# Sums of a first expert pass moved from the attention stage into the pass, for 12 of 16 chunks, with the attention stage's first work in the pass's last blocks

## The chip, the cores and the metric

One NeuronCore of one Trainium2 chip. The time is device microseconds of one execution of the whole program. The kernel before has a median of 1704.45 us over three runs (1703.83 to 1704.88).

## What is computed

8192 tokens of 256 features go through a layer norm and a mixture-of-experts block, a layer norm and a spectral attention, and the same expert block again:

```python
def ffn(x):                       # 8 experts, top 2 of a sigmoid router
    shared = silu(xf @ sw1) * (xf @ sw3) @ sw2
    h = gelu(einsum('nd,edh->neh', xf, ew1))
    y = einsum('neh,ehd->ned', h, ew2)
    return shared + einsum('ned,ne->nd', y, comb)
def attn(x):
    q, k, v = x @ Wq.T, x @ Wk.T, x @ Wv.T
    fk, fq = unit(rfft(k)), unit(rfft(q))
    fkv = cumsum(fk * rfft(v), axis=tokens)
    return x + irfft(fkv * conj(fq))
x = x + 0.5 * ffn(layernorm(x))
x = x + attn(layernorm(x))
x = x + 0.5 * ffn(layernorm(x))
```

## The kernel before, in words

The tokens stay in SBUF as `X`, 64 tiles of 128 rows; four tiles are a chunk, so there are 16 chunks (`CH`). The program is written as one instruction stream for each engine, with semaphores between them, and with loops by `run_steps` that peel the first and last steps. Each stream runs the same stages: stage A, stage B, attention, stage A, stage B.

Stage A (`steps_a`) does the shared expert and the router chunk by chunk and scatters each normalised row, with its number, into the list of its expert in DRAM (`lists`).

Stage B (`phase_b`) is the routed experts, the "pass" of this text: 71 pairs of 128-row blocks (`PAIRS`), in an order that follows the tokens, so that the results of early chunks are complete early. For each pair SyncE loads 256 list rows into one of four buffers `XB` (line 345), TensorE transposes them (846), ScalarE and VectorE split them and the expert's weights into a high and a low part, TensorE multiplies in three products (710 to 712), ScalarE applies gelu (616), TensorE multiplies again two steps later, VectorE copies the result out of its bank (1238, `YB`), and GpSimd scatters the rows to `results` in DRAM with two indirect DMAs (453). The instructions of step s on one engine belong to pairs s + 2 (rows and weights), s (first product and gelu) and s − 2 (second product and copy out).

The second pass also adds the results to the tokens. In its step n SyncE waits for the scatter of pair n − 10 and for the sum of tile n − 23, and loads the two results of each token of tile n − 20 into one of four buffers `YT` (`last_part`, line 363). In step n VectorE adds tile n − 19: two multiply-adds of 128x256 (`last_tile`, 1249). ScalarE adds a shift to each tile there, and SyncE stores finished chunks.

The first pass does none of this. Its results are added in the attention stage. There SyncE waits for all scatters (`results_in`), then loads a chunk's results, 1 MB, into the one buffer `YG` (`load_results`, 383). VectorE's attention step s adds chunk s + 2 with eight multiply-adds (1294) and takes its statistics (981, 985). GpSimd makes mean and inverse deviation of them (`rstd_of`, 404 to 418), ScalarE normalises the chunk (676), TensorE transposes it (924), ScalarE and VectorE split it (`XA`), and TensorE makes the spectra of k, v and q of chunk s (710 to 712 on `t_xah`, `t_wfh`). VectorE multiplies k and v spectra, TensorE takes prefix sums over the tokens (934, 936), VectorE multiplies them with the spectrum of q (1326, 1327, 1329), GpSimd finishes the complex product and scales it (499 to 505), TensorE transposes (911) and transforms back (946), and VectorE adds it to `X` (1277).

The order on an engine is as written; nothing is rearranged. Steps −2 and −1 of attention are the start: sums, statistics, normalisation and transposes of chunks 0 and 1. The products of the weights with the Fourier matrix (`attention_weights`, 884) stand on TensorE between the pass and step −1, all twelve in a row:

```python
for i in range(3):
    for m in range(KD):
        for k in range(KD):
            ins = pe.matmul(bank[:, 2 * i + m, 0:D], raw_w[i][:, k, m * P:(m + 1) * P],
                            raw_fwd[:, k, :], start=(k == 0), stop=(k == KD - 1))
```

The raw weights `raw_w` lie where the second pass keeps `YT`; `XN`, `YG` and the other attention buffers lie over stage B's.

## Time and profile before

| what | value |
|---|---|
| median of the runs | 1704.45 us |
| profiled execution, its own time | 1685.51 us |
| its span, first to last instruction | 1683.7 us |
| mean granted TensorE clock | 0.959 |
| PE busy | 1447.3 us (86%) |
| DVE busy | 1289.2 us (77%) |
| ACT busy | 925.0 us (55%) |
| POOL busy | 858.8 us (51%) |
| DMA read and written | 108 GB/s over the span |

Busy times are sums over stages with different limits, so they don't say what a stage waits for. For that the trace is read stage by stage: as windows, which give each engine's busy time in a stretch, and as a timeline, where a row is start, duration, engine, line, operation and operands, and in brackets the idle time before it with what ended it. PE is TensorE, DVE VectorE, ACT ScalarE, POOL GpSimd, SPq the DMA queue of SyncE. A clock of 1.00 is TensorE's full speed.

### The profile page before, as it was taken

How to read it: one execution, taken by the hardware profiler on the slowest of the kernel's cores; microseconds unless marked ns; L12 is line 12 of the kernel's file. 1: busy time of each engine (PE TensorE's matmuls, PEld its weight loads, DVE VectorE, ACT ScalarE, POOL GpSimd, SP SyncE). 2: the span in 40 equal slices, each digit the busy share in tenths (PEclk: the TensorE clock that was granted, in tenths of full speed). 3: DMA queues.
4: the chain of work that ended last, by engine and by line, in shares of the span. 5: the costliest groups of instructions: out<-in, count | busy, mean ns of one | idle time of the engine just before them, and what ended most of it. 6: DMA issues, size and time to landing. Idle time of an engine off the chain costs nothing.

```text
span 1683.7 us, 34493 instructions
## 1 busy us (share of the span) xinstructions
PE 1447.3 (86%) x9656; PEld 1294.3 (77%) x9657; DVE 1289.2 (77%) x3361; ACT 925.0 (55%) x1435; POOL 858.8 (51%) x1056
## 2 busy tenths in 40 slices
PE   1899999998999987688888886999999998999994
PEld 0677777777999887678777775777777788989994
DVE  4788888876666665789999867788888776689887
ACT  3333333335666554688888886333333325677772
POOL 0444444442555554356666655554444432566664
PEclk9999999999999998789999997999999998999997
DMA  8411111124554444311111110111111124578887
GB/s 286 154 50 50 50 51 48 52 69 142 150 152 143 151 140 132 99 29 53 49 51 51 43 38 0 52 53 51 49 48 51 49 77 139 157 235 263 257 255 232
DMA packets 107704, 176.98 MB, mean 105 GB/s; under 512 B 13360, under 2 KB 72632, under 8 KB 107320
## 3 DMA queue, kind: packets, MB, share of 16 engines
q1 hardware_dynamic: 81704, 104.16, 21.7%
q0 software_dynamic: 25920, 71.86, 11.5%
q8 instruction: 37, 0.61, 0.2%
q14 instruction: 43, 0.35, 0.1%
HBM read 95.75 MB, written 86.70 MB: 108 GB/s over the span
## 4 chain that ended last, share of the span: by engine, by line
PE 37%; issue 20%; DVE 16%; POOL 11%; DMA 6%; ACT 5%; SPq 3%; DVEq 1%; another core or an unknown queue 1%; POOLq 0%; ACTq 0%
PE bank L710 10%; PE bank L712 10%; PE bank L711 10%; POOL lists L441 5%; DMA lists<-a_rows,a_slots 3%; PE bank L846 3%; DVE X L1294 2%; ACT a_rows L566 2%; PE bank L946 2%; DVE a_gate_u L1101 2%; ACT a_uh L517 1%; PE bank L934 1%; DVE a_gate_u L1103 1%; DVE a_xtl L974 1%
## 5 line engine op out<-in xcount | busy, mean ns | idle before, releaser
L453 POOL DMA_INDIRECT results<-b_yb,b_goal x284 | 306.9, 1081 | 247.1 <-DVE b_yb L1238 158.1
L441 POOL DMA_INDIRECT lists<-a_rows,a_slots x256 | 256.7, 1003 | 148.5 <-issue 107.5
L517 ACT ACTIVATE a_uh<-a_gate_u 128x512 fp32r<-128x512 f32 x128 | 77.0, 625 | 228.5 <-PE bank L712 196.1
L710 PE MATMUL bank<-a_sw2h,a_uh 128*128 128x256 f32 x512 | 154.5, 302 | 54.0 <-DVE a_xtl L974 41.3
L710 PE MATMUL bank<-b_xbth,b_w1h 128*128 128x256 f32 x568 | 172.8, 304 | 3.6 <-issue 3.3
L710 PE MATMUL bank<-ew_h,b_hth 128*128 x568 | 162.3, 286 | 2.7 <-issue 2.4
L711 PE MATMUL bank<-b_xbtl,b_w1h 128*128 128x256 f32 x568 | 161.5, 284 | 2.9 <-issue 2.7
L712 PE MATMUL bank<-b_xbth,b_w1l 128*128 128x256 f32 x568 | 161.3, 284 | 2.8 <-issue 2.6
L712 PE MATMUL bank<-ew_h,b_htl 128*128 x568 | 160.8, 283 | 2.3 <-issue 2.3
L711 PE MATMUL bank<-ew_l,b_hth 128*128 x568 | 160.8, 283 | 1.8 <-issue 1.8
L974 DVE TENSOR_TENSOR b_htl<-b_hb,b_hth 128x512 fp32r<-128x512 f32 x142 | 97.8, 689 | 80.8 <-ACT b_hth L517 67.5
L711 PE MATMUL bank<-a_sw2l,a_uh 128*128 128x256 f32 x512 | 148.5, 290 | 0.0
L712 PE MATMUL bank<-a_sw2h,a_ul 128*128 128x256 f32 x512 | 148.4, 290 | 0.0
L710 PEld LDWEIGHTS bank<-a_sw2h,a_uh 128*128 128x128 f32 x512 | 101.8, 199 | 60.3 <-DVE a_xtl L974 47.0
L535 ACT ACTIVATE a_gate_u<-bank 128x512 f32<-128x512 f32 x128 | 75.9, 593 | 126.3 <-DVE a_ul L974 74.7
L517 ACT ACTIVATE b_xbth<-bank 128x512 fp32r<-128x512 f32 x142 | 83.7, 589 | 96.4 <-remote 50.0
L710 PE MATMUL bank<-t_wfh,t_xah 128*128 128x256 f32 x384 | 116.1, 302 | 7.6 <-DVE t_xal L974 7.6
L1238 DVE COPY b_yb<-bank 128x512 f32<-128x512 f32 x142 | 97.1, 684 | 32.7 <-remote 29.3
L974 DVE TENSOR_TENSOR a_ul<-a_gate_u,a_uh 128x512 fp32r<-128x512 f32 x128 | 85.0, 685 | 45.6 <-ACT a_uh L517 44.8
L434 POOL COPY a_rows<-tok 128x2 f32 (+1 forms) x64 | 12.3, 193 | 205.3 <-DVE a_slots L1094 205.2
L616 ACT ACTIVATE b_hb<-bank 128x512 f32<-128x512 f32 x142 | 83.9, 591 | 57.9 <-PE bank L712 35.7
L1101 DVE TENSOR_TENSOR a_gate_u<-a_gate_u,bank 128x512 f32<-128x512 f32 x128 | 87.7, 685 | 35.2 <-ACT a_gate_u L535 31.8
(211 smaller groups left out, 4858.3 us busy)
## 6 DMA issues: line engine op xcount, KB each, us to landing
b_xb<-lists SPq DMA_DIRECT2D x142, 264.0 KB
t_yg<-results SPq DMA_DIRECT2D x16, 1024.0 KB, 5.4
b_yt<-results SPq DMA_DIRECT2D x64, 256.0 KB
X<-in_L_attn_x SPq DMA_DIRECT2D x16, 512.0 KB
out<-X SPq DMA_DIRECT2D x16, 512.0 KB
results<-b_yb,b_goal POOLq DMA_INDIRECT x284
lists<-in_c_fill SPq DMA_DIRECT2D x16, 264.0 KB
w_raw_ew<-in_L_ffn_ew SPq DMA_DIRECT2D x2, 2048.0 KB, 13.8
```

The source lines that it names most:

```text
L441: pool.indirect_dma_start(out=lists, out_offset=bass.IndirectOffsetOnAxis(ap=slots[:, q, k, j:j + 1], axis=0), in_=rows[:, q, j, :], in_of ...
L453: pool.indirect_dma_start(out=results, out_offset=bass.IndirectOffsetOnAxis(ap=goal[:, u, blk:blk + 1], axis=0), in_=YB[:, u % 4, blk, :], ...
L517: return act.activation(o, i, ACT.Copy)
L535: act.activation(gate_u[:, m % 2, :], bank[:, 2 + 2 * (m % 2), :], ACT.Sigmoid).then_inc(s_sig, 1)
L616: act.activation(HB[:, par], bank[:, 2 + par, :], ACT.Gelu).then_inc(s_gelu, 1)
L710: pe.matmul(o, a("h"), b("h"), start=first, stop=False)
L711: pe.matmul(o, a("h"), b("l"), start=False, stop=False)
L712: return pe.matmul(o, a("l"), b("h"), start=False, stop=last)
L846: ins = pe.transpose(bank[:, 1 - par, (2 * k + blk) * P:(2 * k + blk + 1) * P], XB[:, slot, blk, k * P:(k + 1) * P], ident)
L974: return dve.tensor_tensor(o, v, h.bitcast(F32), ALU.subtract)
L1101: ch.link(dve.tensor_tensor(gu, gu, bank[:, 2 + 2 * (m % 2), :], ALU.mult))
L1238: dve.tensor_copy(YB[:, slot].rearrange("p b d -> p (b d)"), bank[:, 6 + par, :]).then_inc(s_yok, 1)
```

## The change

`EARLY = 12`. The first pass now loads and adds the results of the first 12 chunks (48 tiles) as the second pass does, without ScalarE's shift and without stores. The attention stage loads and adds chunks 12 to 15 alone; VectorE still takes the statistics of every chunk there, but for chunks 0 and 1. Those have their statistics in steps 67 and 68 of the pass, GpSimd's `rstd_of` after the scatters of pairs 66 and 68, and ScalarE's normalisation into buffers of their own: chunk 0 in ScalarE's step 69, ahead of the last pair's gelu, chunk 1 behind the pass. TensorE's weight products stand in its steps 70 (v, and k once the last gelu has read its bank), 72 (q, once the last result is copied out), the transposes of chunk 0 in step 71. The raw weights are loaded after the last of the 48 tiles is added, since they use its buffers. ScalarE waits for all scatters before its first attention step.

```diff
+EARLY = 12
+WEIGHT_BANK = [2, 4, 6]
-DVE_A, DVE_T, POOL_T, ACT_T = 86, 36, 20, 8
+DVE_A, DVE_T, POOL_T, ACT_T = 86, 22, 20, 8
...
+        XN_FIRST = [place("t", f"xn{i}", [P, J, D], F32, where["yg"] + 4 * i * J * D) for i in range(2)]
+        XAL_FIRST = place("t", "xal_first", [P, KD, N], F32R, where["fq"] + 4 * J * D)
...
-                    if layer:
-                        last_part(n, slot, q)
+                    last_part(n, slot, q)
                 def last_part(n, slot, q):
+                    tiles = TILES if layer else EARLY * J
...
-                        sp.wait_ge(s_ysc[done], (q + (slot + 2) // 4) * 32 + (YW[done] - 32 * (WAY // 4 + 1) + 32))
+                        sp.wait_ge(s_ysc[done], (q + (slot + 2) // 4) * 32 + (YW[done] * layer - 32 * (WAY // 4 + 1) + 32))
-                    if inside(n - LOAD - 4, TILES):
-                        sp.wait_ge(s_fc, n - (LOAD + 3))
+                    if inside(n - LOAD - 4, tiles):
+                        sp.wait_ge(s_fc, n - (LOAD + 3) + EARLY * J * layer)
-                        if slot == 3:
+                        if layer and slot == 3:
...
-                if layer == 0:
-                    run_steps(sp, step, 0, 4, PAIRS - 3, PAIRS, 4)
-                else:
-                    run_steps(sp, step, 0, LOAD + 4, PAIRS - 3, TILES + LOAD + 4, 4)
+                run_steps(sp, step, 0, LOAD + 4, PAIRS - 3, (TILES if layer else EARLY * J) + LOAD + 4, 4)
...
-            run_steps(sp, load_results, 0, 2, CH, CH, 2)
+            sp.dma_start(WI[:], c_inv.rearrange("(k p) n -> p k n", p=P)).then_inc(s_inv, 16)
+            sp.wait_ge(s_atp, 2)
+            for c in range(EARLY, CH):
+                atleast(sp, s_comb, c - EARLY)
+                sp.dma_start(YG[:].rearrange("p j k d -> p j (k d)"), res_d[:, c * J:(c + 1) * J, :]).then_inc(s_yg, 16)
...
+                    if layer == 0 and isinstance(n, int) and n in (PAIRS - 5, PAIRS - 3):
+                        c = (n - (PAIRS - 5)) // 2
+                        rstd_of(c, CH + c + 1, c)
...
+                    if layer == 0 and isinstance(s, int) and s == PAIRS - 2:
+                        act.wait_ge(s_rstd, CH + 1)
+                        act.wait_ge(s_bps, PAIRS - 1)
+                        act.wait_ge(s_goal, PAIRS - 1)
+                        normalised(0, 0, XN_FIRST[0])
...
+            act.wait_ge(s_mm1, PAIRS)
+            attention_weights(0, 1)
+            attention_weights(1, 0)
+            act.wait_ge(s_atp, 1)
+            copy(XA["h"][:], bank[:, 0:2, :]).then_inc(s_ah, 1)
+            act.wait_ge(s_rstd, CH + 2)
...
+            normalised(1, 1, XN_FIRST[1])
+            attention_weights(2, 2)
+            for i in range(4):
+                act.wait_ge(s_ysc[i], YW[i])
-            run_steps(act, attention, -2, 4, CH - 2, CH, 2, ca, ACT_T)
+            run_steps(act, attention, 0, 4, CH - 2, CH, 2, ca, ACT_T)
...
+                    if layer == 0 and isinstance(s, int) and s == PAIRS - 1:
+                        pe.wait_ge(s_mat, 64)
+                        attention_weights(1)
+                        pe.wait_ge(s_gelu, PAIRS)
+                        attention_weights(0)
+                    if layer == 0 and isinstance(s, int) and s == PAIRS:
+                        pe.wait_ge(s_txn, 1)
+                        transposed(XN_FIRST[0])
+                    if layer == 0 and isinstance(s, int) and s == PAIRS + 1:
+                        pe.wait_ge(s_yok, PAIRS)
+                        attention_weights(2)
...
-                    if inside(s - ADD, TILES):
+                    if inside(s - ADD, TILES if layer else EARLY * J):
                         last_tile(s, u, q)
+                    if layer == 0 and isinstance(s, int) and s in (PAIRS - 4, PAIRS - 3):
+                        stats(s - (PAIRS - 4), s - (PAIRS - 4))
+                    if layer == 0 and isinstance(s, int) and s == PAIRS:
+                        weights_low(0, 1)
+                        weights_low(1, 0)
+                    if layer == 0 and isinstance(s, int) and s == PAIRS + 1:
+                        dve.wait_ge(s_ah, 1)
+                        dve.wait_ge(s_yps, PAIRS - 1)
+                        low(XAL_FIRST[:], bank[:, 0:2, :], XA["h"][:]).then_inc(s_al, 1)
...
-                if far:
+                if far and isinstance(s, int) and s + 2 >= EARLY:
                     c = s + 2
-                    dve.wait_ge(s_yg, c * 16 + 16)
+                    dve.wait_ge(s_yg, (c - EARLY) * 16 + 16)
...
-                    stats(c, par)
+                if far:
+                    stats(s + 2, par)
...
-            run_steps(dve, attention, -2, 4, CH - 2, CH, 2, ch, DVE_T)
+            run_steps(dve, attention, 0, 4, EARLY - 2, CH, 2, ch, DVE_T)
```

VectorE, the end of a step in the loop of the first pass: `b_htl` is the low part of the gelu's output, `b_yb` the result copied out, `b_goal` the row numbers, `b_yt` a tile's loaded results. Before:

```order
L1218 ISA x2
L1220 ISA [waits h1_ps]
L1220 COPY b_w1l<-ew_l 128x512
L974 TENSOR_TENSOR b_htl<-b_hb,b_hth 128x512 [waits ht_h]
L1238 COPY b_yb<-bank 128x512 [waits y_out1,y_ps]
L1240 CAST b_goal<-b_xb 128x2
L1213 REGISTER_ALU
```

Now:

```order
L1012 TENSOR_TENSOR b_htl<-b_hb,b_hth 128x512 [waits ht_h]
L1276 COPY b_yb<-bank 128x512 [waits y_out1,y_ps]
L1278 CAST b_goal<-b_xb 128x2
L1285 REGISTER_ALU
L1288 ISA [waits f_in0]
L1288 SCALAR_TENSOR_TENSOR X<-b_yt_108,gates,X 128x256
L107 REGISTER_ALU
L1288 ISA [waits dve_chain]
L1288 SCALAR_TENSOR_TENSOR X<-b_yt_108,gates,X 128x256
```

Two multiply-adds stand behind the result's copy, the first behind a wait for the tile's load, the second behind a wait for the first.

ScalarE, from the last but one pair of the first pass on: `b_hb` is the gelu, `b_hth` its high part, `t_wfh` the high part of a weight product, `t_xn` a normalised chunk, `t_xah` its transposed high part. Before:

```order
L616 ACTIVATE b_hb<-bank 128x512 [waits ht_l,h1_ps]
L517 ACTIVATE b_hth<-b_hb 128x512 [waits y_ps,gelu_ok]
L616 ACTIVATE b_hb<-bank 128x512 [waits ht_l,h1_ps]
L517 ACTIVATE b_hth<-b_hb 128x512 [waits y_ps,gelu_ok]
L517 ACTIVATE t_wfh<-bank 128x256 [waits mat_ps] x6
L676 ACTIVATE t_xn<-X,shift,rstd 128x256 [waits rstd_ok]
L676 ACTIVATE t_xn<-X,shift,rstd 128x256 x3
L517 ACTIVATE t_xah<-bank 128x1024 [waits a_xt_ps]
```

Now:

```order
L638 ACTIVATE t_xn_102<-X,shift,rstd 128x256 [waits goal_ok,xb_ps,rstd_ok]
L638 ACTIVATE t_xn_102<-X,shift,rstd 128x256 x3
L616 ACTIVATE b_hb<-bank 128x512 [waits ht_l,h1_ps]
L517 ACTIVATE b_hth<-b_hb 128x512 [waits y_ps,gelu_ok]
L517 ACTIVATE t_wfh<-bank 128x256 [waits mat_ps,h1_ps]
L517 ACTIVATE t_wfh<-bank 128x256 [waits mat_ps] x3
L517 ACTIVATE t_xah<-bank 128x1024 [waits a_xt_ps]
L638 ACTIVATE t_xn_103<-X,shift,rstd 128x256 [waits goal_ok,xb_ps,rstd_ok]
L638 ACTIVATE t_xn_103<-X,shift,rstd 128x256 x3
L517 ACTIVATE t_wfh<-bank 128x256 [waits mat_ps] x2
L651 ACTIVATE t_sq<-bank 128x1024 [waits y_out3,y_out2,k_ps,y_out1,y_out0]
```

Chunk 0 is normalised ahead of the last pair's gelu, and the first square of the attention stage waits for the four scatter semaphores besides its spectrum.

VectorE, from the copy of pair 68 on: `t_wfl` and `t_xal` are low parts, `t_yg` is a chunk's loaded results. Before:

```order
L1238 COPY b_yb<-bank 128x512 [waits y_out0,y_ps]
L1238 COPY b_yb<-bank 128x512 [waits y_out1,y_ps]
L1238 COPY b_yb<-bank 128x512 [waits y_out2,y_ps]
L974 TENSOR_TENSOR t_wfl<-bank,t_wfh 128x256 [waits mat_hi] x6
L1294 SCALAR_TENSOR_TENSOR X<-t_yg,gates,X 128x256 [waits dve_chain,yg_in]
L1294 SCALAR_TENSOR_TENSOR X<-t_yg,gates,X 128x256 x3
```

Now:

```order
L1276 COPY b_yb<-bank 128x512 [waits y_out0,y_ps]
L1276 COPY b_yb<-bank 128x512 [waits y_out1,y_ps]
L1012 TENSOR_TENSOR t_wfl<-bank,t_wfh 128x256 [waits mat_hi] x4
L1276 COPY b_yb<-bank 128x512 [waits y_out2,y_ps]
L1012 TENSOR_TENSOR t_xal_first<-bank,t_xah 128x1024 [waits y_ps,a_xt_h]
L1012 TENSOR_TENSOR t_wfl<-bank,t_wfh 128x256 [waits mat_hi] x2
```

The low parts of the weights stand between and behind the last copies, chunk 0's low part is there before the attention steps, and no sum stands behind them.

## Rows read from the trace of the kernel before

**Rows 1.** Timeline, DVE: copies of pairs 0, 19, 57, 70, both passes
```profile
407.53 0.68 DVE L1238 COPY b_yb<-bank 128x512 f32<-128x512 f32 x1
...
474.24 0.68 DVE L1238 COPY b_yb<-bank 128x512 f32<-128x512 f32 x1
...
615.93 0.69 DVE L1238 COPY b_yb<-bank 128x512 f32<-128x512 f32 x1
...
657.33 0.69 DVE L1238 COPY b_yb<-bank 128x512 f32<-128x512 f32 x1 [1.03 <-issue]
...
1415.87 0.68 DVE L1238 COPY b_yb<-bank 128x512 f32<-128x512 f32 x1
...
1485.46 0.68 DVE L1238 COPY b_yb<-bank 128x512 f32<-128x512 f32 x1
...
1619.70 0.68 DVE L1238 COPY b_yb<-bank 128x512 f32<-128x512 f32 x1
...
1663.49 0.69 DVE L1238 COPY b_yb<-bank 128x512 f32<-128x512 f32 x1 [0.61 <-remote]
```

**Rows 2.** Windows, pairs 19 to 57, both passes: busy us (instructions), PEclk, DMA share
```profile
474.00:616.00 142.00, 134.07 (x1082) 129.87 (x1081) 90.72 (x192) 86.24 (x154) 79.16 (x77) 0.99 0.48 143
1485.00:1620.00 135.00, 126.96 (x1054) 123.56 (x1053) 122.91 (x268) 104.06 (x190) 89.38 (x76) 1.00 0.86 259
```

**Rows 3.** Source view, line 1249, second pass: ns min/median/max
```profile
L1249 DVE SCALAR_TENSOR_TENSOR X<-b_yt,gates,X x128: 471/484/487, 1479.6 to 1679.7; 128x256 f32 x72, 128x256 f32<-128x256 f32 x56
```

**Rows 4.** Timeline, all engines, 651 to 688 us: the pass to the spectrum
```profile
651.86 1.44 POOL L453 DMA_INDIRECT results<-b_yb,b_goal  x1 [2.31 <-DVE b_yb L1238]
...
652.78 0.60 ACT L616 ACTIVATE b_hb<-bank 128x512 f32<-128x512 f32 x1 [1.04 <-PE bank L712]
...
657.13 3.19 PE L884 MATMUL bank<-b_raw_fwd,b_raw_w 128*128 128x256 f32 x14
...
663.76 0.96 POOL L453 DMA_INDIRECT results<-b_yb,b_goal  x1 [0.31 <-issue]
...
665.64 0.39 ACT L517 ACTIVATE t_wfh<-bank 128x256 fp32r<-128x256 f32 x1 [1.75 <-remote]
...
672.01 3.38 DVE L1294 SCALAR_TENSOR_TENSOR X<-t_yg,gates,X 128x256 f32<-128x256 f32 x8 [5.53 <-DMA t_yg<-results]
...
677.09 0.38 DVE L985 BATCH_NORM_AGGREGATE mv<-st 128x2 f32<-128x6 f32 x4 [0.15 <-DVE st L981]
...
680.35 2.07 ACT L676 ACTIVATE t_xn<-X,shift,rstd 128x256 f32<-128x256 f32 x4 [14.32 <-POOL shift_a L418]
...
682.48 1.97 PE L924 MATMUL bank<-cst,t_xn 128*128 128x128 f32 x8 [20.00 <-ACT t_xn L676]
...
686.17 1.19 DVE L974 TENSOR_TENSOR t_xal<-bank,t_xah 128x1024 fp32r<-128x1024 f32 x1
...
687.51 0.55 PE L710 MATMUL bank<-t_wfh,t_xah 128*128 128x256 f32 x1 [3.07 <-DVE t_xal L974]
```

**Rows 5.** Timeline, DVE, line 1329, one product each attention step
```profile
742.52 1.23 DVE L1329 TENSOR_TENSOR t_fq<-bank,t_fq 128x1024 f32<-128x1024 f32 x1
...
763.64 1.22 DVE L1329 TENSOR_TENSOR t_fq<-bank,t_fq 128x1024 f32<-128x1024 f32 x1
...
784.63 1.23 DVE L1329 TENSOR_TENSOR t_fq<-bank,t_fq 128x1024 f32<-128x1024 f32 x1
...
805.59 1.22 DVE L1329 TENSOR_TENSOR t_fq<-bank,t_fq 128x1024 f32<-128x1024 f32 x1
...
973.88 1.23 DVE L1329 TENSOR_TENSOR t_fq<-bank,t_fq 128x1024 f32<-128x1024 f32 x1
...
993.65 1.23 DVE L1329 TENSOR_TENSOR t_fq<-bank,t_fq 128x1024 f32<-128x1024 f32 x1
```

**Rows 6.** Timeline, DVE, line 1294, eight sums within one step
```profile
790.64 4.57 DVE L1294 SCALAR_TENSOR_TENSOR X<-t_yg,gates,X 128x256 f32 x4
795.37 1.92 DVE L1294 SCALAR_TENSOR_TENSOR X<-t_yg,gates,X 128x256 f32 x4 [0.15 <-DVE X L1294]
```

More of the change, by code:

```diff
@@ L490, in attention @@
                     meanwhile()
-                if far:
+                if far and not (isinstance(s, int) and s < 0):
                     rstd_of(par, s + (CH + 3), s + 2)
@@ L821, in steps_a, with attention_weights, transposed @@
                 return step
+            def attention_weights(i):
+                for m in range(KD):
+                    for k in range(KD):
+                        ins = pe.matmul(bank[:, WEIGHT_BANK[i] + m, 0:D], raw_w[i][:, k, m * P:(m + 1) * P],
+                                        raw_fwd[:, k, :], start=(k == 0), stop=(k == KD - 1))
+                    ins.then_inc(s_mps, 1)
+            def transposed(xn):
+                for k in range(KD):
+                    for j in range(J):
+                        ins = pe.transpose(bank[:, k, j * P:(j + 1) * P], xn[:, j, k * P:(k + 1) * P], ident)
+                ins.then_inc(s_atp, 1)
             def phase_b(layer):
@@ L921, in attention @@
                     atleast(pe, s_ph, s - 1)
[L922 to L925 removed]
+                    transposed(XN_FIRST[1] if isinstance(s, int) and s == 0 else XN)
                 if prev:
@@ L938, in attention @@
                 if old:
+                    if isinstance(s, int) and s == 2:
+                        pe.wait_ge(s_inv, 16)
                     pe.wait_ge(s_ph, s - 1)
```

80 lines of the change are left out of this document (33 added, 47 removed).

## The prediction

> **What bounds the kernel now.** I began with the page: TensorE is busy for most of the span, so a change matters only where TensorE waits or where another engine sets the pace. Then I read the two expert passes and the attention stage between them apart, since their limits differ.
>
> In the expert passes TensorE sets the pace. The source view of the copy that ends a pair gives the clock of a pass: the first pass takes 657.33 − 407.53 = 249.8 us for 71 pairs, the second 1663.49 − 1415.87 = 247.6 us [rows 1]. The windows over pairs 19 to 57 say why this is a good comparison [rows 2]. In the first pass VectorE is busy 90.7 of 142 us. In the second, which already adds one tile of results per step, it is busy 122.9 of 135 us, and TensorE 127.0 of 135. So the second pass is a full trial of what the change does to the first.
>
> Between the pass and the first spectrum the bound is a chain in which TensorE has nothing to do [rows 4]. The weight products begin at 657.13, the last is copied at 665.64. The loaded results hold VectorE back for 5.53 us, the sums take 3.38, statistics end near 677.5, ScalarE normalises from 680.35 (it had waited 14.32 us), TensorE stands 20.00 us before the transposes at 682.48, and the first spectrum starts at 687.51. That is 687.51 − 657.13 = 30.4 us, of which some 10 are TensorE work.
>
> In the attention stage one product per step marks the cadence [rows 5]: 21.12, 20.99 and (784.63 to 805.59) 20.96 us. In the steady steps that is VectorE in order: the eight sums take 795.37 + 1.92 − 790.64 = 6.65 us of each [rows 6]. At 973.88 a step starts that has no sums, because no chunk is left; it takes 993.65 − 973.88 = 19.77 us. So taking 6.65 us from VectorE saves little over 1 us of time: the next limit is a ring of the product, GpSimd's four multiplications, TensorE's transposes, two spectra and prefix sums, and back to the product.
>
> **The change part by part.**
>
> *Start of attention.* Two chunks' loads, sums, statistics and normalisation leave the chain; the weight products stay on TensorE but stand between the last pairs. Count forward from the first pass's end. GpSimd scatters pair 66 from 651.86, and the last ten scatters fill 651.86 to 664.72, 1.29 us each [rows 4]; so pair 66 is out near 654.5. Then its new work for chunk 0 follows; before, ScalarE started 680.35 − 677.09 − 0.30 ≈ 2.9 us after the statistics' last part, so 657.4. ScalarE's normalisation takes 2.07, to 659.5. The last pair's gelu, before at 652.78, is queued behind it on ScalarE: it is 6.7 us late, and its high and low parts (0.6 us for the gelu, a like time for each part) end near 661.3. TensorE has meanwhile done the first four weight products (a third of 657.13 to 665.6, so 2.8 us) and idles some 3 us for that gelu; then 2.8 for the second third, 1.5 for pair 69, 1.5 for the transposes (1.97 in the row), 1.5 for pair 70, 0.7 for the copy, 2.8 for the last third: 660.2 + 2.8 + 1.5 + 1.5 + 1.5 + 0.7 + 2.8 = 671.0. The 1.5 for a pair's second product is an estimate: a pair of 3.5 us is two such products and a few transposes. ScalarE's and VectorE's parts of chunk 0 (VectorE's is 1.19) are done beside this. The first spectrum starts at 671 to 674 instead of 687.51: 13.5 to 16.5 us less; I take **15**. The ends: if GpSimd and ScalarE were never late, TensorE work alone would end at 657.1 + 8.5 + 1.5 = 667 (20 us less); if the weights' load, which now waits for the last tile's sum because it shares its buffers, or the statistics in steps 67 and 68 (1.8 us each on VectorE) push TensorE back by 3 us, and GpSimd is 3 us later, 677 (10 less).
>
> *Scatters.* GpSimd's two new pieces delay the last four pairs' scatters by up to 5.8 us, to about 670.5. ScalarE's first square now waits for them all, but needs the first spectrum anyway: 24 products, as many as a pair has, so 3.5 us at least, to 675. It costs nothing, with some 3 us of cover for the landing of the last scatter; what goes beyond counts one for one.
>
> *Attention steps.* The sums leave the steps for chunks 2 to 11, ten steps. The first two start-up steps are led by ScalarE and gain nothing. In the next two, the one of 21.12 among them, VectorE waited for TensorE before the product, so they were on the ring already: nothing. The six after that go from 20.97 to the ring's length, 1.2 us less by the bare step of 19.77, and a little more in every second one, which has one prefix product fewer: **8 us**. At the least 4, if the statistics and GpSimd's piece for the chunk to come, which the bare step lacks, lie in the ring; at the most ten steps of 1.4, 14. Chunks 12 to 15 keep their sums and their 20.96, and their loads now start long before they are wanted: zero.
>
> *Sums in the pass.* 48 tiles of two sums: 96 × 0.484 = 46.5 us of VectorE [rows 3] in a pass where it has 142 − 90.7 = 51 idle over pairs 19 to 57 alone. The same 38 pairs take 1619.70 − 1485.46 = 134.2 us in the second pass against 615.93 − 474.24 = 141.7 in the first [rows 1]: with sums they are 7.5 us faster, not slower. I don't know why the first pass has a slower last part, so I do not count on losing it. The second pass's first 19 pairs are 2.9 us slower (69.6 against 66.7), which may be its longer code or its own extra work. I take **3 us less**, with the ends 10 less and 8 more.
>
> The trace holds a warning about one cost that would count against this placing. The first four sums in a step take 4.57 us, the next four 1.92, so 1.14 against 0.48 us for the same instruction; the slow ones stand beside GpSimd's two-input operations. In the second pass, beside GpSimd's scatters, the sum is 0.484 at the median and 0.487 at most [rows 3], while a scatter grows from 79.16/77 = 1.03 to 89.38/76 = 1.18 us [rows 2]. The Trainium skill (SBUF — State Buffer, Who Contends for the ports) has VectorE instructions with two SBUF inputs contend with a GpSimd instruction that reads SBUF, the second to issue blocking until the first ends. By it, with each scatter held for a whole sum, a pair would need 2 × (1.29 + 0.484) = 3.55 us of GpSimd, as long as a pair lasts, and the 3 us of the pass would go from the sum. The trace shows a hold of 0.15 us per scatter, a third of a sum: two scatters at 1.29 + 0.15 make 2.9 us per pair, under 3.5, so it stays hidden.
>
> *Sum.* 15 + 8 + 3 = 26 us. The profiled execution has a span of 1683.7 and its own time of 1685.5; the median of the runs is 1704.45, 19 us above it, and I take the difference off the median: **1678 us**.
>
> **The rivals.**
>
> *A, 54%:* as above, 1678.
>
> *B, the steps don't get shorter, 15%:* the statistics, which stay, and what they start on GpSimd keep the ring at 21. For: two of the steps with sums were already on the ring. Against: the bare step of 19.77. 1704.45 − 15 − 3 = 1686.
>
> *C, the pass takes on the second pass's rhythm, 14%:* 7 to 8 us instead of 3 there, and the start at its better end: 1704.45 − 8 − 8 − 18 = 1670.
>
> *D, the start gains half, 8%:* the late gelu, the weights' load and the scatters add up, 7 us instead of 15: 1686. It would show as TensorE idle over 8 us near the weight products.
>
> *E, slower, 5%:* the queue of list loads. SyncE now waits in each step, ahead of the next pair's load, for the scatter of ten pairs before and for the sum of the tile 23 steps before. If VectorE, over 90% busy, falls behind, loads start late, TensorE waits, and VectorE waits for TensorE in turn. It ends slower when it eats the other parts' 23 us and 3.4 more, 0.55 us on each of 48 pairs: 3.73 (141.7/38) becoming 4.28. Against: the second pass has the same queue with output stores on top, DMA share 0.86, and 3.53 per pair. At 4.4 it would give 1704.45 + 32 − 23 = 1713.
>
> *F, no effect beyond the noise, 4%:* the same, stopping at about 4.2 per pair: 1704. A measurement of this kernel tells some 0.2%, 3.4 us, from no change.
>
> The Trainium skill (DMA: Bandwidth & Descriptors, Bandwidth) asks for transfers of 1 MiB or more, against the 256 KiB loads that take the place of twelve of 1 MiB. By its fit of 2.0 us plus size, four small ones cost 10.4 us where one large costs 4.4, an estimate from that page; the sum would change only if they were waited for, and the fit has no wait in it. That mechanism is rival E.
>
> **How the numbers follow.** Forecast 1678. A's own range is 1668 to 1688 by the ends above, not all met at once. B, C and D lie inside 1664 to 1691; leaving out E, F and the tails of A and B is under 2 in 10. Faster 0.91 (A to D), same 0.04 (F), slower 0.05 (E).
>
> **What would show it.** Right: from pair 57's copy to the first spectrum 55 to 58 us where it was 687.51 − 615.93 = 71.6; TensorE's longest idle moment there 3 to 4 us, before the products that need the last gelu, not 20; six steps at 19.3 to 19.8 us and four at 21; the 71 pairs in 240 to 252 us; scatter rows near 1.15 us. Wrong: pairs above 4 us, list loads that TensorE waits for in the first pass, steps still at 21 without sums, or a square that waits for scatters.

## The result, and the profile after

| | before | after |
|---|---|---|
| median of four runs each | 1704.14 us (1703.08 to 1704.88) | 1655.93 us (1649.84 to 1668.29) |
| ratio, 95% interval | | 0.9748 [0.9709, 0.9788] |
| span of the profiled execution | 1683.7 us | 1666.5 us |
| PE, DVE busy | 1447.3, 1289.2 us | 1446.4, 1263.3 us |

The change gains 48 us, 22 more than forecast, and the time lies outside the range of 1664 to 1691. The profiled execution of the changed kernel is its slowest, and that of the kernel before lies 18 us under its timed runs, so their spans differ by 17 us only. Places are therefore read here, not totals, and both kernels were taken again (below).

Timeline, DVE: the copies of pairs 0, 19, 57 and 70 in both passes, as [rows 1].

```profile
410.07 0.68 DVE L1276 COPY b_yb<-bank 128x512 f32<-128x512 f32 x1
...
478.70 0.68 DVE L1276 COPY b_yb<-bank 128x512 f32<-128x512 f32 x1
...
609.67 0.69 DVE L1276 COPY b_yb<-bank 128x512 f32<-128x512 f32 x1
...
660.13 0.69 DVE L1276 COPY b_yb<-bank 128x512 f32<-128x512 f32 x1 [0.27 <-PE bank L733]
...
1382.76 0.68 DVE L1276 COPY b_yb<-bank 128x512 f32<-128x512 f32 x1
...
1460.78 0.68 DVE L1276 COPY b_yb<-bank 128x512 f32<-128x512 f32 x1
```

Pairs 19 to 57, which carry the sums, take 131.0 us instead of 141.7. Pairs 0 to 19 of the second pass, which the change doesn't touch, take 78.0 us instead of 69.6: something varies by 8 us on its own.

Windows over those pairs, as [rows 2], and the source view of the sums, as [rows 3]:

```profile
479.00:609.00 130.00, 125.76 (x1049) 123.22 (x1050) 120.86 (x265) 88.92 (x151) 88.60 (x76) 1.00 0.79 231
```

```profile
L1288 DVE SCALAR_TENSOR_TENSOR X<-b_yt,gates,X x224: 470/483/490, 472.9 to 1662.5; 128x256 f32 x72, 128x256 f32<-128x256 f32 x40
```

VectorE is busy 120.9 of 130 us, the sums cost 0.483 us as forecast, and a scatter 88.60/76 = 1.17 us on average.

Timeline, all engines, from the pass to the attention stage, as [rows 4]:

```profile
646.68 1.89 PE L847 MATMUL bank<-b_raw_fwd,b_raw_w 128*128 128x256 f32 x8
...
650.15 2.07 ACT L638 ACTIVATE t_xn<-X,shift,rstd 128x256 f32<-128x256 f32 x4 [5.88 <-POOL shift_a L415]
...
652.13 0.57 ACT L616 ACTIVATE b_hb<-bank 128x512 f32<-128x512 f32 x1
...
652.75 3.12 PE L847 MATMUL bank<-b_raw_fwd,b_raw_w 128*128 128x256 f32 x8 [4.18 <-ACT b_hb L616]
...
657.65 1.03 PE L854 MATMUL bank<-cst,t_xn 128*128 128x128 f32 x8
...
660.88 1.99 PE L847 MATMUL bank<-b_raw_fwd,b_raw_w 128*128 128x256 f32 x8 [0.78 <-DVE b_yb L1276]
...
662.52 0.47 PE L731 MATMUL bank<-t_wfh,t_xah 128*128 128x256 f32 x1
...
664.87 0.96 POOL L450 DMA_INDIRECT results<-b_yb,b_goal  x1 [0.30 <-issue]
...
667.42 1.02 ACT L651 ACTIVATE t_sq<-bank 128x1024 f32<-128x1024 f32 x1 [4.12 <-DMA results<-b_yb,b_goal]
```

The forecast's picture is there: the normalisation waits for GpSimd, the last gelu stands behind it, TensorE waits 4.18 us for that gelu. From pair 57's copy to the first spectrum it is 662.52 − 609.67 = 52.9 us, against 71.6 before. The first square waits for the scatters, which the forecast had called covered. It comes 4.8 us after the first spectrum, against 5.0 us before, so this wait adds nothing here.

Timeline, DVE, the product of each attention step, as [rows 5]: three in a row.

```profile
754.80 1.22 DVE L1383 TENSOR_TENSOR t_fq<-bank,t_fq 128x1024 f32<-128x1024 f32 x1
...
775.94 1.23 DVE L1383 TENSOR_TENSOR t_fq<-bank,t_fq 128x1024 f32<-128x1024 f32 x1
...
795.78 1.23 DVE L1383 TENSOR_TENSOR t_fq<-bank,t_fq 128x1024 f32<-128x1024 f32 x1
```

Steps without sums alternate: 21.14 and 19.84 us. Windows over the same place in two neighbouring steps show why. Columns: busy PE, PEld, DVE, ACT, POOL, then PEclk.

```profile
760.00:762.00 2.00, 0.06 (x1) 0.00 (x0) 2.00 (x5) 1.90 (x2) 2.00 (x3) 1.00 0.00 0
...
763.00:764.00 1.00, 1.00 (x7) 1.00 (x6) 0.00 (x0) 0.99 (x2) 0.92 (x3) 0.50 0.00 0
...
781.00:783.00 2.00, 0.43 (x4) 0.23 (x2) 2.00 (x5) 1.53 (x2) 2.00 (x2) 1.00 0.00 0
...
784.00:785.00 1.00, 1.00 (x11) 1.00 (x10) 0.00 (x0) 0.60 (x1) 0.99 (x2) 1.00 0.00 0
```

In both steps TensorE stands for some 2 us (2.01 and 1.77) until GpSimd has finished the product. In the first, the granted clock is 0.50 (1.2 GHz) right behind that, and one us holds 7 matmuls instead of 11; in the second it stays at 1.00 (2.4 GHz).

### The profile page after: what moved, and what is told of

The parts are those of the page before. It is cut to its first block, busy times and chain, and to the rows that moved or that the text cites. A ratio compares the mean times of both kernels' runs of the same rounds, so it can differ in the third digit from the quotient of the medians.

```text
span 1666.5 us, 34750 instructions
## 1 busy us (share of the span) xinstructions
PE 1446.4 (87%) x9656; PEld 1293.6 (78%) x9657; DVE 1263.3 (76%) x3361; ACT 927.6 (56%) x1435; POOL 854.6 (51%) x1056
## 4 chain that ended last, share of the span: by engine, by line
issue 25%; PE 25%; DVE 14%; POOL 12%; SPq 9%; ACT 7%; DMA 6%; another core or an unknown queue 1%; ACTq 0%; POOLq 0%; DVEq 0%
PE bank L731 7%; PE bank L733 6%; PE bank L732 6%; POOL lists L438 6%; DMA lists<-a_rows,a_slots 3%; ACT a_rows L566 2%; SPq L348 2%; SPq L367 2%; SPq L349 2%; DVE a_gate_u L1139 2%; PE bank L985 2%; DVE X L1347 2%; PE bank L880 1%; DMA b_xb<-lists 1%; ACT a_uh L517 1%
## 5 line engine op out<-in xcount | busy, mean ns | idle before, releaser
L450 POOL DMA_INDIRECT results<-b_yb,b_goal x284 | 314.4, 1107 | 247.2 <-DVE b_yb L1276 147.2
L616 ACT ACTIVATE b_hb<-bank 128x512 f32<-128x512 f32 x142 | 84.0, 592 | 73.1 <-PE bank L733 51.8
L1288 DVE SCALAR_TENSOR_TENSOR X<-b_yt,gates,X 128x256 f32 (+1 forms) x224 | 107.1, 480 | 18.0 <-DMA b_yt<-results 6.1
L431 POOL COPY a_rows<-tok 128x2 f32 (+1 forms) x64 | 12.2, 190 | 208.3 <-DVE a_slots L1132 208.2
```

The source lines that it names most:

```text
L450: pool.indirect_dma_start(out=results, out_offset=bass.IndirectOffsetOnAxis(ap=goal[:, u, blk:blk + 1], axis=0), in_=YB[:, u % 4, blk, :], ...
L616: act.activation(HB[:, par], bank[:, 2 + par, :], ACT.Gelu).then_inc(s_gelu, 1)
L1288: ins = dve.scalar_tensor_tensor(xt, YT[slot][:, k * D:(k + 1) * D], gates[:, k, bass.ds(t, 1)], xt, ALU.mult, ALU.add)
```

## The experiments

**Both kernels again, one part alone, and a quarter of the sums.** Four kernels side by side; the kernel before took 1703.61 us beside them, and the ratios are to that.

> The kernel before, unchanged, to see where an ordinary execution of it spends the 19 us by which the median lay above the profiled one. Theory R (rhythm): they lie in the expert passes, so this profile, if its time is near 1704, has 71 pairs of the first or the second pass in 258 us or more, with pairs of about 4.0 us, and the attention stage as before (first product at line 1329 to the last 312 us). Theory S (start and steps alone explain the gain): passes of 247 to 251 us, and the 19 us elsewhere. Ratio 1.00.

> The changed kernel, unchanged. Theory R: the first pass is again 248 to 252 us in every profile, with pairs of 3.35 us where tiles are summed, and what differs between executions is the second pass (248 to 265). Theory S: the first pass varies as much as the second. Ratio 0.965 to 0.978.

`sums_only` moves the sums and leaves statistics, normalisation, transposes and weight products of the start behind the pass:

```diff
-                    if layer == 0 and isinstance(s, int) and s in (PAIRS - 4, PAIRS - 3):
-                        stats(s - (PAIRS - 4), s - (PAIRS - 4))
...
-            run_steps(dve, attention, 0, 4, EARLY - 2, CH, 2, ch, DVE_T)
+            run_steps(dve, attention, -2, 4, EARLY - 2, CH, 2, ch, DVE_T)
```

> Only the sums of 12 chunks moved; statistics, normalisation, transposes and weight products of chunks 0 and 1 stand behind the pass as before. Lost against the changed kernel: the interleaved start, of which the wait for loaded results is still gone (13 us of the 25 kept). Theory R: 1704 less 13 (no load and sum at the start), 6 (steps) and about 18 (a regular first pass), 1667. Theory S: 1704 - 13 - 6 = 1685.

`three_chunks` keeps the new start and moves three chunks (the loops that this touches are adapted, which is left out here):

```diff
-EARLY = 12
+EARLY = 3
```

> The start as changed, but sums of only 3 chunks in the pass (tiles in steps 19 to 30); the other 13 chunks are summed in attention steps. Theory R: the pass keeps its irregular rhythm from step 31 on, so 1704 less 25 (start) is 1679, with a first pass as in the kernel before. Theory S: the first pass does not matter, the start gives 25 and the steps nothing: 1679 too, but then sums_only is 1685. The attention steps are back at 20.96 us.

| | median us | ratio to before |
|---|---|---|
| b_again | 1700.25 | 0.9985 [0.9956, 1.0014] |
| a_again | 1660.15 | 0.9755 [0.9722, 0.9788] |
| sums_only | 1668.37 | 0.9802 [0.9769, 0.9836] |
| three_chunks | 1674.29 | 0.9835 [0.9801, 0.9868] |

sums_only takes 1668 us, where theory R said 1667 and theory S 1685; three_chunks, for which both said 1679, takes 1674. The profiles of b_again and a_again (spans 1699.6 and 1659.3 us) are a fair pair. Between the copies of pairs (p) and the products of the attention steps:

| stretch, us | b_again | a_again | difference |
|---|---|---|---|
| p0 to p19 | 68.0 | 71.7 | +3.7 |
| p19 to p57 | 148.7 | 131.3 | −17.4 |
| p57 to first product | 103.1 | 83.9 | −19.2 |
| first to last product | 312.5 | 308.0 | −4.5 |
| last product to second pass | 382.7 | 382.2 | −0.5 |
| second pass, p0 to p70 | 253.5 | 251.9 | −1.6 |

So 17 us come out of the pass itself, where the change only adds work. Moving the sums alone brings it (sums_only has 130.5 us for p19 to p57); with three chunks the pairs come evenly in steps 19 to 30 alone (134.9 us for all 38). Here is what stands in these pairs. View of waits, TensorE, 480 to 600 us, of b_again; then of the changed kernel:

```profile
PE bank L710 <- issue: 4.1, 5, 1.1
PE bank L712 <- issue: 3.5, 5, 1.1
PE bank L711 <- issue: 2.8, 6, 1.0
```

```profile
PE bank L880 <- DMA b_xb<-lists: 2.7, 4, 0.9
PE bank L880 <- issue: 0.8, 3, 0.4
```

In the kernel before TensorE stands 10.4 us between matmuls of one and the same product, with nothing that the profile shows to wait for. Timeline of b_again, one such place, four matmuls that follow one another:

```profile
491.75 0.37 PE L712 MATMUL bank<-b_xbth,b_w1l 128*128 128x256 f32 x1 [0.43 <-issue]
493.18 0.36 PE L710 MATMUL bank<-b_xbth,b_w1h 128*128 128x256 f32 x1 [1.06 <-issue]
493.88 0.28 PE L711 MATMUL bank<-b_xbtl,b_w1h 128*128 128x256 f32 x1 [0.34 <-issue]
494.63 0.36 PE L712 MATMUL bank<-b_xbth,b_w1l 128*128 128x256 f32 x1 [0.47 <-issue]
```

They take 2.9 us where such matmuls come every 0.12 us, and they follow two pairs in quick succession: the copies of three pairs lie 2.2, 5.1 and 3.2 us apart (10.5), and at times 2.2, 2.3 and 7.7 (12.2) with the stalls in the last. With sums nearly all copies come every 3.2 to 3.8 us, and the stalls are gone.

The 10.4 us are not all that is lost. The view counts moments without any matmul of over 0.15 us; a matmul that starts late while the one before still counts as busy is not in it. Added up from start to start inside the products, beyond 0.12 us each, the late starts of pairs 19 to 57 make 26.6 us in b_again (18.0 in the first profile of the kernel before) and 3.1 in a_again. The change has some 5 us more outside the products, where TensorE waits ahead of its transposes, in part for list loads. The difference, 23.5 − 5, is about the 17.4 us of the table. Twice in these pairs of b_again the clock falls right behind a group of stalls; in a_again it stays at 1.00 between 485 and 617 us. Windows, b_again, one group of stalls (TensorE busy 1.6 of 4 us) and what follows it:

```profile
536.00:540.00 4.00, 1.60 (x11) 1.24 (x10) 0.60 (x1) 1.11 (x2) 2.26 (x3) 1.00 0.50 173
541.00:543.00 2.00, 2.00 (x11) 2.00 (x11) 1.28 (x4) 1.95 (x4) 0.00 (x0) 0.50 0.01 4
```

Behind the group the clock is 0.50 for some 3 us, and the matmuls start 0.21 us apart instead of 0.12.

**Is it the pace?** Useless work in the place of the sums, and the sums' loads without the sums. The kernel before took 1688.66 us beside these, on the same chip as in the runs above.

```diff
+                def evenly():
+                    for k in range(2):
+                        ch.settle()
+                        ch.link(dve.scalar_tensor_tensor(pace[:], pace[:], gates[:, k, 0:1], pace[:], ALU.mult, ALU.add))
...
-                    if inside(s - ADD, TILES):
-                        last_tile(s, u, q)
+                    if inside(s - ADD, TILES if layer else 48):
+                        if layer:
+                            last_tile(s, u, q)
+                        else:
+                            evenly()
```

> The kernel before, with two more multiply-adds of 128x256 on VectorE in each of steps 19 to 66 of the first pass, on a scratch buffer: no loads, no waits on SyncE, and the real sums stay in the attention stage. Theory P (pace): what the change gained beyond the forecast is that VectorE's two sums per pair hold the pass to an even 3.35 us, so that TensorE no longer runs two pairs in 2.2 us each and then stands without instructions. Then the useless sums do the same: pairs 19 to 57 in 131 to 135 us where the kernel before takes 141.7 to 148.7, and the program takes 1688 us. Theory Q (queue): it is SyncE's waits for the scatter and the tile, which space the loads of the lists. Then pairs 19 to 57 stay at 141 to 149 us, and the program at 1703, or some us more.

`no_sums` leaves the sums out: VectorE counts the tile as done at once.

```diff
+                    if layer == 0:
+                        dve.sem_inc(s_fc, 1)
+                        return
```

> The changed kernel without the 96 sums of the first pass (the results of 48 tiles are left out of the tokens); the loads of the tiles, SyncE's waits and VectorE's waits for the loads stay. Theory P: pairs 19 to 57 go back from 131 to 141 to 149 us, with 12-us triples of pairs, and the program from 1660 to 1672. Theory Q: 131 us and 1660.

`pace_all` calls `evenly()` in steps 0 to 18 of both passes of the changed kernel:

```diff
+                    if isinstance(s, int) and 0 <= s < ADD:
+                        evenly()
```

> The changed kernel with two useless multiply-adds of 128x256 in each of steps 0 to 18 of both passes, where no tile is summed. Theory P: these steps go from 67 to 78 us to 61 to 65 in each pass, and the program from 1660 to 1648 us. Theory Q: more VectorE work with no queue gains nothing: 1660 to 1664.

`pace_before` takes 1671.52 us, 0.9901 [0.9869, 0.9934] of the kernel before: 17 us gained by adding work. Timeline, DVE, the copies of pairs 19 and 57 of pace_before, and of no_sums:

```profile
475.08 0.68 DVE L1239 COPY b_yb<-bank 128x512 f32<-128x512 f32 x1
...
599.95 0.68 DVE L1239 COPY b_yb<-bank 128x512 f32<-128x512 f32 x1
```

```profile
479.98 0.68 DVE L1277 COPY b_yb<-bank 128x512 f32<-128x512 f32 x1
...
618.47 0.68 DVE L1277 COPY b_yb<-bank 128x512 f32<-128x512 f32 x1
```

124.9 us with useless sums and no loads; 138.5 us, with triples of 12 us again, where loads and queue stay and the sums go. no_sums takes 1663.87 us, 0.9881 [0.9836, 0.9926] (the changed kernel was not measured beside it; its ratio elsewhere is 0.9755 and 0.9789). So theory P stands, and theory Q falls as the main cause. Neither forecast of no_sums is met exactly: 138.5 us lies a little under the 141 to 149 of theory P, so a small part by the queue is not excluded. Traffic is no cause either: no_sums has a DMA share of 0.73 in these pairs, b_again 0.46, and its stalls are no worse (5.5 us against 10.4 in the same view; late starts 14.9 us against 26.6, and 3.1 in pace_before):

```profile
PE bank L732 <- issue: 2.5, 5, 0.8
PE bank L733 <- issue: 1.6, 5, 0.4
PE bank L734 <- issue: 1.4, 4, 0.4
```

pace_all takes 1644.51 us, 0.9737 [0.9706, 0.9767]. Steps 0 to 18 take 61.5 us in either pass, as expected; in clock_fill (below), measured beside it without this work, they take 69.1 and 70.0. By ratio alone the interval overlaps a_again's, so the gain is read from these stretches.

**Any engine, or VectorE alone?** In the kernel before, on a second chip (1691.47 us there), two useless ScalarE operations per step:

```diff
+                    if not layer and inside(s - ADD, 48):
+                        for k in range(2):
+                            ce.settle()
+                            ce.link(act.activation(pace[:], cst[:, 0:D], ACT.Identity))
```

> The kernel before with two useless ScalarE operations of 128x256 in each of steps 19 to 66 of the first pass. Theory P (pace): any engine that TensorE must wait for each pair keeps it from running ahead; ScalarE has 96 us of work over 142, and with 38 times two more it holds the pairs as VectorE did: pairs 19 to 57 in 125 to 135 us, 14 us less than before in the same call. Theory V (VectorE alone): the two-input sums on VectorE hold GpSimd's scatters back by the port that they share and so thin out the transfers; ScalarE's work does not, and the pass stays as before.

1674.71 us, 0.9910 [0.9880, 0.9940]; pairs 19 to 57 in 129.8 us. Theory P again: ScalarE's work gives 17 us too, so VectorE's two-input sums are not needed for it, and theory V falls. ScalarE's work doesn't remove the stalls altogether: in the view of waits of 480 to 600 us 3.0 us of them are left, with VectorE's useless sums none.

**Attention: is it the clock?** Measured beside pace_all:

```diff
+                if old and now:
+                    atleast(pe, s_vused, s)
+                    for i in range(10):
+                        pe.matmul(bank[:, 4, 0:D], XA["h"][:, 0, 0:P], WF["h"][:, 0, 0, :], start=True, stop=True)
                 if old:
                     pe.wait_ge(s_p, s - 1)
```

> The changed kernel with ten useless products of 128x256 on TensorE between the spectrum of k and the transposes of the product in each attention step from the third on, where TensorE stands 1.8 to 2.2 us. Theory K (clock): every second step without sums takes 21.14 instead of 19.84 us because the granted clock is 0.50 for 3 us behind that idle time; with the filler it stays 1.00, all of steps 2 to 8 take 19.8, and the program 1655 to 1656. Its rival, theory N: the ring itself alternates with the prefix sums, which have one product fewer in every second step, and the slow products are hidden: 21.14 and 19.84 stay, and the program takes 1660.

1649.34 us, 0.9763 [0.9730, 0.9797]. Its timeline, DVE, the same three products, and the windows behind the filler:

```profile
754.98 1.23 DVE L1387 TENSOR_TENSOR t_fq<-bank,t_fq 128x1024 f32<-128x1024 f32 x1
...
774.63 1.22 DVE L1387 TENSOR_TENSOR t_fq<-bank,t_fq 128x1024 f32<-128x1024 f32 x1
...
794.48 1.23 DVE L1387 TENSOR_TENSOR t_fq<-bank,t_fq 128x1024 f32<-128x1024 f32 x1
```

```profile
761.00:762.00 1.00, 0.45 (x4) 0.24 (x3) 1.00 (x4) 1.00 (x2) 1.00 (x1) 1.00 0.00 0
762.00:763.00 1.00, 0.73 (x7) 0.73 (x8) 0.79 (x6) 0.98 (x2) 1.00 (x2) 1.00 0.00 0
763.00:764.00 1.00, 1.00 (x11) 1.00 (x10) 0.00 (x0) 0.99 (x2) 1.00 (x2) 1.00 0.00 0
```

19.65 and 19.85 us instead of 21.14 and 19.84, and the clock stays at 1.00: theory K. First to last product takes 300.8 us, against 305.1 in pace_all and no_sums, measured beside it, and 306 to 308 in the changed kernel's profiles. The ratio of the whole program, 0.9763, doesn't show these 4 to 7 us: the changed kernel has 0.9755 and 0.9789 elsewhere. They are shown in the stretch alone.

**The start: gelu or scatters?** With the changed kernel as the measure beside it, on the second chip (before 1691.47 us):

> The changed kernel once more, as the measure for the next kernels of this call: 0.972 to 0.979 of the kernel before by every theory. In the last call the kernel before ran at 1689 us instead of 1704; if the stalls of TensorE in the first pass are what varies from call to call (theory P), the changed kernel's lead is smaller where the kernel before is fast, 0.977 to 0.98.

```diff
-                    if layer == 0 and isinstance(s, int) and s == PAIRS - 2:
+                    if layer == 0 and isinstance(s, int) and s == PAIRS - 1:
                         act.wait_ge(s_rstd, CH + 1)
```

> The changed kernel with chunk 0's normalisation on ScalarE behind the last pair's gelu instead of ahead of it. Theory G (gelu): TensorE stands 4.18 us before the second third of the weight products because that gelu is queued behind a normalisation that waits for GpSimd; behind it, TensorE stands under 1.5 us there, the transposes of chunk 0 wait for nothing new, and the start is 3 to 4 us shorter: from pair 57's copy to the first spectrum 48 to 50 instead of 51.2 to 52.9 us, 3 us less in all. Its rival, theory H: the chain of GpSimd's deviation, the normalisation and the transposes sets the start anyway, and the time stays within 1 us.

> The changed kernel with the useless sums in steps 0 to 18 of both passes (pace_all), the ten filler products in the attention steps (clock_fill) and the late normalisation (late_norm). If the three act in different places and add up: 10 to 14, 4 to 5 and 3 us less than the changed kernel in the same call, 18 us in all. If pace_all's gain came from TensorE's clock or from the end of the pass, they overlap, and 12 us or less are left.

| | median us | ratio to before |
|---|---|---|
| a_third | 1653.48 | 0.9789 [0.9758, 0.9820] |
| late_norm | 1657.86 | 0.9813 [0.9783, 0.9842] |
| all_three | 1633.72 | 0.9675 [0.9644, 0.9706] |

late_norm gains nothing: 4 us more than a_third, with overlapping intervals. Its timeline at that place:

```profile
658.23 0.47 PE L731 MATMUL bank<-t_wfh,t_xah 128*128 128x256 f32 x1
...
663.62 0.96 POOL L450 DMA_INDIRECT results<-b_yb,b_goal  x1 [0.30 <-issue]
...
666.17 1.02 ACT L651 ACTIVATE t_sq<-bank 128x1024 f32<-128x1024 f32 x1 [4.35 <-issue]
```

The first spectrum comes 46.4 us after pair 57's copy instead of 51.4, but the first square stands behind the last scatter in both, and the first product comes after 83.0 and 82.8 us. So TensorE's 4.18 us wait for the gelu costs nothing: the last scatter is later. all_three takes 19.8 us less than a_third, so the gains of pace_all and clock_fill add up.

Then chunk 1's deviation was put behind the last scatters. late_both has this, late_norm's edit, and ScalarE's copies of the last weight products ahead of chunk 1's normalisation; best has all of it and pace_fill's edits:

```diff
-                    if layer == 0 and isinstance(n, int) and n in (PAIRS - 5, PAIRS - 3):
-                        c = (n - (PAIRS - 5)) // 2
+                    if layer == 0 and isinstance(n, int) and n in (PAIRS - 5, PAIRS - 1):
+                        c = (n - (PAIRS - 5)) // 4
```

> The changed kernel as the measure for the other three of this call: 0.975 to 0.980 of the kernel before.

> late_norm, and besides GpSimd makes the deviation of chunk 1 behind the last pair's scatters instead of ahead of pair 69's, and ScalarE copies the last weight products before it normalises chunk 1. Theory W (scatters): late_norm brought the first spectrum forward by 5 us and gained nothing because ScalarE's first square waits for the last scatter, which stands behind 3.2 us of GpSimd's work for chunk 1. Then the last scatter starts 3 us earlier, the first square 2 to 4 us earlier than in late_norm and the changed kernel, and the time falls by 2 to 4 us against the changed kernel. Its rival, theory X: the start is set by the second chunk, whose deviation is now later; then the first square comes earlier but the first product (spectrum to product, 31 to 37 us) does not, and the time stays.

> pace_all and clock_fill together, with the changed kernel's own normalisation. If late_norm gained nothing in all_three either, this takes 0.9675 of before as all_three did (19.8 us less than the changed kernel); if late_norm cost 4 us there as it did alone, 24 us less; if it gave some, 16.

> pace_fill and late_both together. By theory W 2 to 4 us less than pace_fill, by theory X the same.

| | median us | ratio to before |
|---|---|---|
| before | 1642.24 | |
| a_fourth | 1626.75 | 0.9903 [0.9888, 0.9919] |
| late_both | 1624.06 | 0.9889 [0.9874, 0.9905] |
| pace_fill | 1622.87 | 0.9886 [0.9869, 0.9903] |
| best | 1623.05 | 0.9882 [0.9867, 0.9897] |

These ran on a third chip, and there both kernels are faster and the gain is 15.5 us: 0.9903 instead of the 0.975 to 0.980 expected. Nearly all of a_fourth's pairs come evenly, also those without sums. Its timeline, DVE, copies of pairs 0, 19 and 57, and its view of waits, TensorE, 480 to 600 us:

```profile
409.09 0.68 DVE L1276 COPY b_yb<-bank 128x512 f32<-128x512 f32 x1
...
469.79 0.68 DVE L1276 COPY b_yb<-bank 128x512 f32<-128x512 f32 x1
...
600.11 0.68 DVE L1276 COPY b_yb<-bank 128x512 f32<-128x512 f32 x1
```

```profile
PE bank L880 <- DMA b_xb<-lists: 0.7, 2, 0.5
```

19 pairs without sums take 60.7 us here, 3.19 each, where the first pass on the other chips takes 66 to 74; 38 pairs with sums take 130.3 us, 3.43 each, as on the others. So where there are no stalls a pair with a tile costs 0.24 us more. The sums themselves are hardly that: useless ones in the 19 pairs of pace_fill make them 61.6 us instead of 60.7. The rest comes with the loads and their queue, which was not taken apart.

In late_both the first square comes 51.8 us after pair 57's copy (a_fourth 53.9) and the first product 79.4 (81.5), but the third product 122.6 in both: the second step is 21.1 us long instead of 19.5. That step holds a stretch at half clock, and a_fourth's second step has none. Windows, late_both:

```profile
709.00:710.00 1.00, 1.00 (x7) 1.00 (x6) 0.12 (x2) 0.99 (x2) 1.00 (x2) 0.50 0.06 16
```

So what is gained at the start and lost there says nothing for theory X: which steps get the slow clock differs from run to run (a_again has 21.1 us there too, a_third 19.5, the same kernel). The filler takes this out of the comparison. Between best and pace_fill the first square comes 2.0 us earlier (51.9 against 53.9), the first product 0.6 us, and the medians are the same, 1623.05 and 1622.87. That is theory X in the time: an earlier first square brings nothing that can be told. pace_fill and best take 4 us less than a_fourth, with intervals that overlap pace_fill's; first to last product is 300.9 us against 307.1, the filler's part, and pace_fill's first 57 pairs take 1.6 us more. What late_norm gives or costs inside all_three, which pace_fill was to tell, stays open, since here the pacing has no stall to take away.

**The kernel before on one more chip**, to see the stalls' part. On this fourth chip it takes 1700.43 us.

> The kernel before on another chip. In the last call, on a chip of its own, it took 1642 us and the changed kernel 1627, and no pass of the changed kernel had a triple of pairs of 12 us. Theory P: what varies from chip to chip is TensorE's stalls without a releaser. Where the program takes 1642 us, the first pass has none: 3.2 to 3.3 us per pair from the first one on, 38 pairs from 19 to 57 in 124 to 130 us; where it takes 1690 to 1704, they are there: 140 to 149 us. Rival, theory D: the difference lies in transfers or another stage, and the first pass takes 140 us or more on any chip.

> The kernel before with the useless sums on VectorE in steps 19 to 66 of the first pass, beside b_third on its chip. Theory P: where the kernel before takes 1690 us or more, 17 us less; where it takes 1642, there is no stall to take away, and it gains nothing or loses up to 4 us.

b_third: 1700.97 us, 1.0012 [0.9979, 1.0045]; p0 to p19 71.3 us and p19 to p57 142.1, with triples. pace_before_2: 1678.88 us, 0.9869 [0.9828, 0.9909], p19 to p57 125.9 us, 22 us gained. Theory P for such chips; the case of a chip without stalls was not met again. The kernel before has no profile from the chip where it takes 1642 us, so that its first pass has no stalls there is concluded from the changed kernel's pairs, not shown.

## Why the prediction was wrong

- **First pass, the term "sums in the pass", forecast −3 us (ends −10 and +8): the step that failed.** It measured −11 (profiled executions, 141.7 to 131.0) to −17 us (b_again to a_again) over pairs 19 to 57. The term put the slow last part of the first pass at nothing to be won. The rows were read rightly: with sums the second pass's pairs were 7.5 us faster. The text then said "I don't know why the first pass has a slower last part, so I do not count on losing it". TensorE's own matmuls in pairs 19 to 57 of the profile at hand would have answered it: 18.0 us of late starts inside products, 5.8 us of them as waits that nothing releases in 480 to 600 us. They follow pairs at which TensorE has run ahead. More work on VectorE for every pair keeps it from running ahead, and the stalls are gone; the second pass, paced in this way, has almost none (0.3 us between 1490 and 1610 us in b_again). Rival C had the outcome, the second pass's rhythm, but no cause, 8 us for it, and 1670 as its time; the measured time is 14 us below that too.
- **The base.** 26 us came off the median with the pass as it was in the profiled execution, whose passes took 249.8 and 247.6 us. In b_again they take 259.3 and 253.5. So an execution 19 us under its median showed less of the stalls than the runs that were to be forecast.
- **Start, forecast −15 us (ends 10 and 20): right in kind, 4 us short.** From pair 57's copy to the first product it is 103.1 to 83.9, so 19.2. The first spectrum came 52.9 us after pair 57's copy, not 55 to 58. In the forecast's own count the last gelu ends 44.3 us after that copy (660.2 − 615.93) and the spectrum comes 10.8 us behind it; measured, 43.0 and 9.8 us. Of the second, TensorE's last third of the weight products was put at 2.8 us, a third of a row's stretch that ended with ScalarE's copy; it took 662.52 − 660.88 = 1.6.
- **Scatters, "it costs nothing": right in the sum, wrong as a picture.** The first square waits for them (4.12 us, released by the DMA), one of the forecast's own signs of being wrong. But it comes 4.8 us behind the first spectrum, 5.0 before the change, so there was no cost; the 3 us of cover were not there, and late_norm, whose spectrum is 5 us earlier, has its first square only 1.6 us earlier.
- **Attention steps, forecast −8 us (ends 4 and 14): −4.5.** The ring is 19.8 us as read from the bare step, but only every second of the six steps reached it; the others take 21.1. What was missed is that TensorE, with VectorE out of the way, stands before the transposes, and in every second step gets a clock of 0.50 for some 3 us: 1.3 us given back. clock_fill removes just that.
- **Rival E** is there in small: TensorE waits 2.7 us for list loads between 480 and 600 us (1.2 in a_again). Scatters of 1.17 us, against a forecast of about 1.15, and sums of 0.483 us were right; no sum in the pass is held for the time of a scatter. The 1 MiB loads of the kernel before took 5.4 us from issue to landing (median), where the forecast's estimate was 4.4. The forecast's "hold of 0.15 us per scatter" is a mean over two kinds, though. Of the 75 scatters of pairs 19 to 57 most take about 1.1 us or less and 25 take 1.3 to 1.5; in pace_before 39 take about 1.0 and 35 take 1.3 to 1.5. By the Trainium skill (SBUF — State Buffer, Who interferes with whom) a VectorE instruction with two SBUF inputs and a GpSimd one that reads SBUF contend, and the second to issue fully blocks. A third of a sum on average doesn't speak against that: single scatters are longer by 0.35 us or more, up to most of a sum of 0.48, others hardly at all. Which of them a sum held is not shown, since 9 of 76 take 1.3 us or more without sums too. What stands is that GpSimd had room for it.

On a chip with stalls the parts sum to the result: −17 −19 −5 +4 and small ones make −40, the difference of the spans of b_again and a_again; by medians the change gained 38 to 48 us there. On the chip without stalls, −19 −5 and 48 × 0.24 = +11 make −13, an estimate from profiles of several chips, against −15.5 measured. The term for the pass, −3, fits neither kind of chip: it is −17 on one and, by this estimate, +11 on the other, and the total of −26 lies between the two results.

## What to carry over

Before a change adds work to an engine with room, look at how the bound engine spends its idle time: if it stands inside its own instruction sequence, a partner that holds it to an even pace can make the stage faster, and a few useless operations show it in one run. If a change takes the last wait off a loop, look at what TensorE then waits for and at the granted clock behind that wait; ten useless products there shortened the attention stage by 4 to 7 us. Take the kernel before on more than one chip when the forecast rests on idle time that no row explains.

## What was new of the hardware

- TensorE stalls without a releaser, up to 1.1 us at a time, 6 to 10 us in 120, after pairs that run at 2.2 us each; with all late starts 18 to 27 us in 38 pairs. They vanish when VectorE holds each pair to 3.3 us, shrink to 3 us in 120 with ScalarE, and a DMA share of 0.73 instead of 0.46 doesn't add to them. No run here shows what TensorE waits for. That TensorE's supply of instructions runs dry is a guess. The trace records transfers of instructions as well (queues q8 and q14), and in b_again none of them lies between 477 and 625 us, while the stalls go on.
- They differ between chips or between times: the same kernel before takes 1689 to 1704 us on three chips and 1642 on another, a distance that is larger than what the whole change gains on the latter. The chip is not all of it: one of the three gave 1704 and, later, 1689 us, and the fast chip was used once.
- At the end of the pass's loop of steps, the changed kernel's copies of pairs 58 and 59 lie 5.1 to 7.1 us apart on the chips with stalls and 3.2 us on the other.
